# A vision tower on one core: both groups of value matmuls ahead of the first score burst, a merged weighing matmul, other PSUM banks and other engine orders

## The reference

```
h = tokens(x)                                # 64 x 197 x 128
h = h + linear_attention(layernorm(h))       # mem_t = q_t @ sum_{s<t} 0.9^(t-1-s) 0.1 k_s v_s^T
routing_input = layernorm(h).mean(axis=1)    # one choice of 3 weight sets per image
sel = argmax(softmax(relu(routing_input @ r_w1 + r_b1) @ r_w2 + r_b2))
h = h + gqa(layernorm(h), *params[sel], nkv) # softmax(q k^T / 4) v, then wo
```

## Time and profile before

| | us |
|---|---|
| median of 3 runs | 851.34 (851.13 to 852.95) |
| the profiled execution | 847.72 |
| its span, first to last instruction | 846.0 |

### The profile page before, as it was taken

The page is one execution under the profiler, slowest core; times in us unless marked ns, Lnnn a source line. Parts: engine busy times, 40 slices in busy tenths (PEclk is TensorE's granted clock), DMA queues, the critical chain, the costliest instruction groups (busy, mean ns, idle before and its releaser), DMA issues.

```text
span 846.0 us, 25937 instructions
## 1 busy us (share of the span) xinstructions
PE 790.8 (93%) x8624; PEld 653.0 (77%) x8624; DVE 602.5 (71%) x1956; ACT 597.9 (71%) x1364; POOL 310.6 (37%) x840
## 2 busy tenths in 40 slices
PE   3778899999999999999999999999999999998996
PEld 3666688888888888888888888888888878876774
DVE  3246777778777786878677777777777777777771
ACT  3556587777777877777787778777777777665664
POOL 1466442443344334433433343343434333431100
PEclk9899999999999999999999999999999999999998
DMA  5555645554545555455455544554455555323220
GB/s 141 149 147 157 197 144 163 155 151 140 170 144 150 147 168 161 130 155 163 146 147 161 161 142 144 169 154 141 145 162 157 146 151 154 98 67 119 95 90 20
DMA packets 138705, 120.55 MB, mean 142 GB/s; under 512 B 12606, under 2 KB 138446, under 8 KB 138574
## 3 DMA queue, kind: packets, MB, share of 16 engines
q1 hardware_dynamic: 136898, 118.34, 47.7%
q10 hardware_dynamic: 1676, 0.57, 0.4%
HBM read 30.99 MB, written 6.46 MB: 44 GB/s over the span
## 4 chain that ended last, share of the span: by engine, by line
PE 71%; DVE 14%; issue 7%; SPq 2%; POOL 2%; DMA 1%; ACT 1%; ACTq 1%; POOLq 1%; DVEq 0%
PE ps L425 11%; PE ps L592 11%; PE ps L543 9%; PE ps L515 4%; DVE top L814 4%; PE ps L569 4%; PE ps L530 3%; PE ps L574 3%; PE ps L624 3%; PE ps L474 3%; PE ps L516 2%; PE ps L484 2%; PE ps L450 2%; DVE mixed L840 2%; PE ps L557 2%
## 5 line engine op out<-in xcount | busy, mean ns | idle before, releaser
L814 DVE TENSOR_REDUCE top<-ps 99x2 f32<-99x394 f32 x512 | 265.6, 560 | 131.9 <-PE ps L543 131.9
L948 ACT ACTIVATE prob<-ps 99x396 f32<-99x396 f32 x512 | 227.2, 496 | 70.2 <-PE ps L574 69.6
L886 ACT ACTIVATE packed<-img 84x686 f32<-84x686 f32 x128 | 177.6, 1394 | 0.5 <-DMA img<-in_x 0.5
L425 PE MATMUL ps<-cols,w_tok 126*128 126x196 f32 x640 | 122.8, 339 | 3.1 <-DMA cols<-packed 2.8
L363 POOL TENSOR_TENSOR var<-mv,eps 99x2 f32<-99x2 f32 x64 | 12.6, 197 | 300.3 <-DVE mv L732 299.9
L543 PE MATMUL ps<-stack 64*99 64x198 f32 x1024 | 110.5, 294 | 7.4 <-DVE top L814 4.0
L569 PE MATMUL ps<-top_rows,pick_rows 64*99 64x198 f32 x1024 | 114.3, 254 | 1.7 <-ACT prob L948 1.5
L543 PEld LDWEIGHTS ps<-stack 64*99 64x99 f32 x1024 | 64.1, 161 | 65.3 <-issue 33.7
L574 PE MATMUL ps<-stack 64*99 64x198 f32 x1024 | 113.4, 252 | 0.0
L592 PE MATMUL ps<-prob,v_ones 99*32 99x198 f32 (+1 forms) x2048 | 112.6, 337 | 0.4 <-ACT prob L948 0.4
L425 PEld LDWEIGHTS ps<-cols,w_tok 126*128 126x128 f32 x640 | 109.0, 196 | 4.3 <-DMA cols<-packed 3.4
(11 more groups left out here) (149 smaller groups left out, 1564.7 us busy)
## 6 DMA issues: line engine op xcount, KB each, us to landing
stack<-qk SPq DMA_DIRECT2D x256, 198.0 KB, 2.5
img<-in_x SPq DMA_DIRECT2D x192, 150.1 KB
cols<-packed SPq DMA_DIRECT2D x128, 160.8 KB
cols<-packed SPq DMA_DIRECT2D x64, 128.6 KB
out<-h SPq DMA_DIRECT2D x64, 49.5 KB
out<-h SPq DMA_DIRECT2D x64, 49.0 KB
w_rows<-in_L_tok_W SPq DMA_DIRECT2D x1, 294.0 KB, 3.2
sets<-in_L_ffn_wo SPq DMA_DIRECT2D x3, 64.0 KB
```

The costliest lines, as they stand in the source:

```text
L425: last = nc.tensor.matmul(ps[:, CX, 0:N * N], w_tok[0:KROWS, s, :], cols[b.ring % 2][:, :, s, :], start=(s == 0), stop=(s == STEPS - 1))
L814: nc.vector.tensor_reduce(top[:, c // 4, first:first + 2], columns, AX.X, ALU.max, negate=True).then_inc(m_read, 1)
L886: last = nc.scalar.activation(packed[b.ring % 2][:, first:end, :], img[b.ring % IMGS][:, :].rearrange("p (x w) -> p w x", w=P)[:, first:en ...
L948: nc.scalar.activation(prob[:, c, :], ps[0:T, E0 + c % 2, 0:CHUNK], ACT.Exp, scale=DK ** -0.5).then_inc(exp_done, 1)
```

## The change

The four shared banks are given out anew (CX router, first attention's first half and top rows; CY patches, q and k, and the output projection; CZ turned patches, v, weighing and `attend_out`; CW masked scores, the second layer norm and all of the mix), and each `wait_ge` that guarded a bank is replaced by one for the bank's new neighbour. `mix_values(b, 0)` and `(b, 1)` both stand at the start of the next slot, ahead of K0, and K0 stands ahead of M0. In `weigh` two matmuls with the same weights, of 99 columns each, become one of 198. The lists of TensorE, VectorE and ScalarE are written in new orders; GpSimd's and SyncE's are as they were, and so are all lists for slots 0 to 11.

```diff
-        M0, E0, MIX, CX, CY, CZ = 0, 2, 4, 5, 6, 7
+        M0, E0, CX, CY, CZ, CW = 0, 2, 4, 5, 6, 7
...
             def weigh(b):
                 pe.wait_ge(att_ready, b.i + 1)
+                topped, patched = b.back(TOPPED - TURNED), b.back(PATCHED - TURNED)
+                if topped.exists():
+                    pe.wait_ge(v_ready, topped.i + 1)
+                elif patched.exists():
+                    pe.wait_ge(h0_ready, patched.i + 1)
                 xhat = xhat1[b.ring % 2]
-                nc.tensor.matmul(ps[:, CY, 0:T], xhat[:, 0, :], att[:, 0:T], start=True, stop=True)
-                nc.tensor.matmul(ps[:, CY, T:SP], xhat[:, 0, :], att[:, T:SP], start=True, stop=False)
-                nc.tensor.matmul(ps[:, CY, T:SP], xhat[:, 1, :], att[:, SP:SP + T],
+                nc.tensor.matmul(ps[:, CZ, 0:SP], xhat[:, 0, :], att[:, 0:SP], start=True, stop=False)
+                nc.tensor.matmul(ps[:, CZ, T:SP], xhat[:, 1, :], att[:, SP:SP + T],
                                  start=False, stop=True).then_inc(u_done, 1)
...
             def project_v(b):
                 pe.wait_ge(wv_copied, b.i + 1)
-                patched = b.back(PATCHED - TOPPED)
-                last_qk = b.back(PROJECTED + 1 - TOPPED)
+                patched, added = b.back(PATCHED - TOPPED), b.back(ADDED - TOPPED)
                 if patched.exists():
                     pe.wait_ge(h0_ready, patched.i + 1)
...
             def mix_values(b, g):
                 if g == 0:
-                    routed = b.back(ROUTED - MIXING)
-                    if routed.ring % BATCH == 0 and routed.exists():
-                        pe.wait_ge(log_ready, batch_of(routed))
                     pe.wait_ge(v_ready, b.i + 1)
-                    if b.has(1):
-                        pe.wait_ge(mix_ready, b.i)
+                    last_added = b.back(ADDED + 1 - ENDING)
+                    if last_added.exists():
+                        pe.wait_ge(x2t_ready, last_added.i + 1)
+                    elif b.has(1):
+                        pe.wait_ge(mixed_t_ready, b.i)
                 pe.wait_ge(exp_done, 8 * b.i + 4 * g + 4)
...
             def project_out(b):
...
-                added = b.back(ADDED - ENDING)
-                if added.exists():
-                    pe.wait_ge(x2t_ready, added.i + 1)
+                projected = b.back(PROJECTED - ENDING)
+                if projected.exists():
+                    pe.wait_ge(lo_ready, projected.i + 1)
+                elif b.has(1):
+                    pe.wait_ge(h2_ready, b.i)
...
                 plan = [
-                    (max_scores, maxed, 0), (key_scores, mixing, 0),
-                    (turn_top, topped), (turn_normed1, turned), (attend_out, added), (patches, patched),
-                    (project_z, turned), (mix_values, ending, 1),
...
-                    (weigh, turned), (mix_values, mixing, 0),
...
+                    (mix_values, ending, 0), (mix_values, ending, 1), (key_scores, mixing, 0),
+                    (max_scores, maxed, 0), (turn_normed1, turned), (attend_out, added), (row_mix, ending),
+                    (project_z, turned), (patches, patched), (turn_mixed, ending), (max_scores, maxed, 1),
+                    (key_scores, mixing, 1), (turn_top, topped), (scores, turned), (turn_patches, patched),
+                    (max_scores, maxed, 2), (key_scores, mixing, 2), (project_qk, projected),
+                    (route_hidden, routing), (project_v, topped), (max_scores, maxed, 3), (key_scores, mixing, 3),
+                    (turn_normed2, added), (route_logits, routing), (weigh, turned), (project_out, ending),
                 ]
...
-                plan = [(choose, choosing), (maximum, maxed, 0), (maximum, maxed, 1), (add_attention, added),
-                        (maximum, maxed, 2), (maximum, maxed, 3), (tokens, patched), (normalise2, added),
...
+                plan = [
+                    (maximum, maxed, 0), (maximum, maxed, 1), (choose, choosing), (normalise, ending),
+                    (add_attention, added), (maximum, maxed, 2), (maximum, maxed, 3), (normalise2, added),
+                    (tokens, patched), (mask_scores, turned), (maximum, maxed, 4), (maximum, maxed, 5),
+                    (route_relu, routing), (measure, patched), (low_halves, projected), (maximum, maxed, 6),
+                    (maximum, maxed, 7), (route_bias, routing), (split_top, maxed), (finish, ending),
+                ]
...
+                plan = [
+                    (keep_mix, ending), (exponent, mixing, 0), (keep_x1t, turned), (exponent, mixing, 1),
...
+                    (exponent, mixing, 6), (exponent, mixing, 7), (keep_u, turned), (pack, arrived, 1),
+                    (route_exp, routing),
+                ]
```

More of the change, by code:

```diff
@@ L406, in _ @@
             for t in range(2):
-                last = nc.tensor.matmul(ps[0:T, CY, t * T:(t + 1) * T], power_wide[:, t, :], ident[0:T, 0:T],
+                last = nc.tensor.matmul(ps[0:T, CZ, t * T:(t + 1) * T], power_wide[:, t, :], ident[0:T, 0:T],
                                         start=True, stop=True)
@@ L500, in route_logits @@
                 for j in range(BATCH):
-                    at = 400 + j * len(KV)
-                    last = nc.tensor.matmul(ps[0:1, MIX, at:at + len(KV)], hidden[:, j:j + 1], r_w2[:, :],
+                    last = nc.tensor.matmul(ps[0:1, CX, j * len(KV):(j + 1) * len(KV)], hidden[:, j:j + 1], r_w2[:, :],
                                             start=True, stop=True)
@@ L550, in turn_top @@
                 pe.wait_ge(split_done, b.i + 1)
-                if b.has(1):
+                routed, turned = b.back(ROUTED + 1 - TOPPED), b.back(TURNED - TOPPED)
+                if turned.exists():
+                    pe.wait_ge(z_ready, turned.i + 1)
+                elif routed.exists() and routed.ring % BATCH == 0:
+                    pe.wait_ge(log_ready, batch_of(routed))
+                elif b.has(1):
                     pe.wait_ge(top_ready, b.i)
-                added = b.back(ADDED - TOPPED)
-                if added.exists():
-                    pe.wait_ge(u_ready, added.i + 1)
                 for t in range(2):
-                    last = nc.tensor.transpose(ps[:, CY, SP + t * T:SP + (t + 1) * T], top_halves[:, t, :], ident[0:T, 0:T])
+                    last = nc.tensor.transpose(ps[:, CX, t * T:(t + 1) * T], top_halves[:, t, :], ident[0:T, 0:T])
                 last.then_inc(top_turned, 1)
@@ L633, in slot @@
                 plan = [
-                    (max_scores, maxed, 0), (key_scores, mixing, 0),
-                    (turn_top, topped), (turn_normed1, turned), (attend_out, added), (patches, patched),
-                    (project_z, turned), (mix_values, ending, 1),
-                    (max_scores, maxed, 1), (key_scores, mixing, 1),
-                    (turn_patches, patched), (scores, turned), (row_mix, ending), (route_hidden, routing),
-                    (max_scores, maxed, 2), (key_scores, mixing, 2),
-                    (turn_normed2, added), (project_v, topped), (route_logits, routing), (turn_mixed, ending),
-                    (weigh, turned), (mix_values, mixing, 0),
-                    (max_scores, maxed, 3), (key_scores, mixing, 3),
-                    (project_qk, projected), (project_out, ending),
+                    (mix_values, ending, 0), (mix_values, ending, 1), (key_scores, mixing, 0),
[5 more added lines that the diff above has]
+                    (turn_normed2, added), (route_logits, routing), (weigh, turned), (project_out, ending),
                 ]
@@ L694, in _ @@
             for k in range(3):
-                last = nc.vector.tensor_reduce(w_shift[:, k:k + 1], ps[:, CX, k * D:(k + 1) * D], AX.X, ALU.add)
+                last = nc.vector.tensor_reduce(w_shift[:, k:k + 1], ps[:, CY, k * D:(k + 1) * D], AX.X, ALU.add)
             last.then_inc(dve_inner, 1)
```

168 lines of the change are left out of this document (83 added, 85 removed).

## The result

The changed kernel takes 865.88 us in the median of 7 runs (865.42 to 870.44), against 851.34 (850.15 to 852.95): the ratio is 1.0175 with an interval of 1.0158 to 1.0192, 14.5 us slower. The forecast was 858.5, 7.2 slower: the side is right and the range holds it, but the loss is twice the one forecast. The profiled execution takes 870.44 us, its span is 868.7.

The account below looks back on a forecast made before the run. TensorE's own list was taken as the bound. Ordinary slots -29.6, `choose` stalls +22.8, slot 14 +2 and drain +12 gave +7.2 on the profiled 847.72; with 3.6 to the median, 858.5 us, range 846 to 867.

Parts of the forecast that it names:

- The ordinary slot: Slot with all steps running, no router batch or `choose`: 12.01 us falls to 11.44, with no new wait.
- the merge: In `weigh`, one matmul of 198 columns for two of 99 saves 0.11 us a slot.
- The change of tile: Adjacent value groups save one change of tile shape and one slow first round: 0.13 us a slot, bounds 0 and 0.24.
- The wait ahead of `turn_normed2`: TensorE's regular wait for `normalise`, 0.33 us a slot, goes because `turn_normed2` now follows K3.
- B: Rival: M3 is late in ordinary slots too, by 0.15 us, making 864.5 us; chance 0.15.
- D: Rival: the merged matmul and the saved change of tile gain nothing, making 871 us; chance 0.05.
- The router's extra: The slot with a router batch stays 0.67 us longer than an ordinary one, bounds 0.4 and 0.9.
- The slot with `choose`: GpSimd's 4.08 us chain from `choose` to `spread2` delays `normalise2` and M3: stall 1.75 us, bounds 0 and 2.2.
- Rival A: The chain on GpSimd behind `choose` doesn't reach M3, so the kernel is faster, 835.7 us; chance 0.15.
- Slot 14's +2: Slot 14, the first with K, has `choose` but no gain from the value groups: +2 us.
- Sum +12, bounds 8 and 16: Drain: slots 71 to 76 +8.4 us, slots 68 to 70 +3, the last two +1.
- the four parts of the table above: Span by `row_mix`: start to image 0, to image 51, to image 63 (drain), to the end.

Follow-up runs that it names:

- e4: The kernel before with only the merged `weigh` matmul (198 columns instead of 99 and 99): 846.12 us against 850.79, ratio 0.994.
- e5: The changed kernel with the first value group moved between `weigh` and `project_out`, apart from the second: 887.98 us, ratio 1.0434 to the kernel before.
- e2: The changed kernel with `choose` back at the head of VectorE's list, ahead of `maximum` 0 and 1: 845.99 us, ratio 0.9965 to the kernel before.
- e11: The kernel before with `choose` moved behind `maximum` 0 and 1: 861.2 us against 852.64, ratio 1.0115.
- e7: The changed kernel with six extra `patches` matmuls on old data per slot from slot 67 on: 855.68 us, ratio 1.0036 to the kernel before.
- e10: The changed kernel with the edits of e2 and e7 joined: 837.09 us, ratio 0.9823 to the kernel before.
- e3: The changed kernel with `turn_mixed` behind M1 and K1 in TensorE's list from slot 69 on: 858.27 us, ratio 1.0083 to the kernel before.
- e6: The changed kernel with the edits of e2 and e3 joined: 839.83 us, ratio 0.9869 to the kernel before.
- e8: The changed kernel with `choose` first and, from slot 69 on, three engines' lists nearly as before: 830.85 us, ratio 0.9752 to the kernel before.

## Why the prediction was right in its direction and wrong in its size

**The ordinary slot: right.** Forecast 11.44, measured 11.44 and 11.43, with no wait on M3. The parts: the merge 0.11 forecast, 0.12 by e4. The change of tile, with the slow first round, 0.13 forecast; 0.19 by e5, inside its bounds. The wait ahead of `turn_normed2` 0.33 is gone. The three would be 0.64 by the measured sizes against the 0.58 that the slot gained, so one of them counts for less when all are together; which isn't settled. Rivals B and D are out.

**The router's extra: 0.79 instead of 0.67,** within its bounds (0.4 to 0.9), 1.6 us in all.

**The slot with `choose`: right in mechanism, somewhat dear.** The chain of 4.08 is 4.13, the wait ahead of `normalise2` is over 1 us and it reaches `project_v` and M3. The stall is mostly 1.45 (17.9 / 13 = 1.37 in the mean, by e2) and not 1.75: 4 to 5 us less. From the start of `normalise2` to M3 it is 2.31 (305.88 to 308.19), with 2.33 forecast; what was taken too long is the stretch from M0's maxima to the end of `choose`, 2.14 (299.57 to 301.71) and not 2.37. That is most of the 0.30. Rival A is out: e2 takes nothing off the chain's work, it only starts it earlier, and the 17.9 that it gives by the ratios is the 17.9 of the thirteen slots.

**Slot 14's +2: not to be read.** The first `row_mix` comes at 119.0 before and 121.0 after, but between 116.1 and 122.8 over all the profiled executions, and at 121.4 and 122.8 in two kernels (e4, e11) whose fill nearly equals that of before.

**The drain: here the forecast failed.** The step is "Sum +12, bounds 8 and 16". It took every duration at full clock and asked of each wait only how long it is; that waiting could change the speed of what stands between the waits was not considered (the trace of the kernel before shows 1.00 up to 840). Measured, in the profiled executions and with slot 66, it is +32.1 where 13.2 were forecast. With the clock held (e7) it is 117.6 - 98.5 = +19.1, so about 13 of the 32 are the clock; in medians the clock is 10 to 12. The Trainium skill ("TensorE: Matmul & The Clock Gate", "A second HAM failure mode: psum-queue depth-cycling") tells of a kernel in which short idle pieces between groups of matmuls were enough to make the clock alternate; the trace of the kernel after agrees: the clock first falls between 756 and 764, behind waits of 0.81 (756.33) and 0.76 (758.53), and is back at 1.00 from 764 to 768.

The 19.1 without the clock, interval by interval: the five up to slot 71 +6.1 (+1.55 of it in slot 66, for which the forecast has 1.2 among the slots; for the other four it has 3), the five up to slot 76 +1.40 to +1.54 each, as forecast (+1.46), and the last two +1.5 and +4.1 where +1 was taken for both. Of that last 4.1 another 1.6 is clock again (e10 has 8.32 there, e7 9.94, before 5.82): e7's clock is 0.67 at 844 to 848.

**The sum, with the clock held.** By the four parts of the table above the forecast is +2, -8.1, +13.2 and 0, together 7.1. In the profiled executions of e7 and of before the parts are +2.9, -11.9, +19.1 and -0.7, together 9.4. So even with the clock held the drain was taken too short: without slot 66 it is +17.6, for which 12 with bounds of 8 and 16 were given, and what was gained beyond the forecast where all steps run (3.8) hides most of that. Their medians are only 4.3 apart (3.1 by the ratio): the profiled execution of the kernel before, from which the drain's 98.5 is read, is 3.6 below its median, that of e7 1.4 above, so 5 of the 9.4 are spread between executions, which goes at least in part with the clock: of 17 runs of the kernel before on one chip, the fastest (848.7) has a mean granted clock of 0.991 and the slowest (854.6) one of 0.983; in e7 853.1 has 0.992 and 857.1 has 0.986. To the 4.3 come the 10.2 of the clock: 14.5. That the range of 846 to 867 holds the result is in part luck: the drain lay outside its own bounds, and gains elsewhere made up for some of it.

**What stays open.** What exactly makes the clock fall. It isn't the longest wait: the kernel before has one of 1.20 in its drain (ahead of a burst at 779.31) and keeps its clock, and e3, with none over 0.92, loses it. The busy times of the stretches don't tell the kernels apart either: the kernel after has 17.65 in the stretch in which the clock falls first, before has 17.02 once and e6 17.08, both at 1.00. In order of what TensorE waits in one drain slot: e7 and e10 0.44, clock 1.00 from 740 to 800; e8 0.97, the same; e6 and e3 1.13, e6 at 1.00 up to 808, e3 falling from 792 on; the kernel after, e2 and e5 1.58 to 1.59, the clock falling before 800 in all three. So more waiting went with more loss, but at 1.13 the same list of TensorE in the drain gave both. No run isolates it further.

## What to carry to other kernels

Work out the ramp and the drain of a pipeline apart, with a list of their own: an order that is good where every step runs may expose each wait once the steps between are gone. Where TensorE is the bound and a change adds waits to it, look at the granted clock too and not at the waits alone; a few idle matmuls in place of a wait are a cheap test of whether the clock is what costs. And look for the engine that is idle just before: a short step that starts a long chain elsewhere belongs ahead of the wait, not behind it.

## What the runs showed of the hardware

- A granted clock that first falls behind waits of TensorE of 0.81 and 0.76 us and is 0.50 (1.2 GHz) from 772 to 788, and six added matmuls per slot that keep it at 1.00 up to 840 and make the kernel 10.2 us faster.
- Executions of one kernel that differ by the clock: in e2 841.6 us at a mean granted clock of 0.976 and 854.9 at 0.956.
- A change of tile shape between 128 and 32 columns costs about 0.19 us, spread over the rows before, in and behind the group.
- Writing a choice and reading it back on GpSimd: 1.09 us from the cast to the first copy, and 0.57 more ahead of the second, while GpSimd shows nothing running (0.81 and 0.40 in e2).
